# Experts of an attention and mixture kernel in four equal steps, both products in three fp32r parts

## The chip, the cores and the metric

One core of a Trainium2 chip runs the kernel. The metric is device microseconds from launch to end, the median of several executions. TensorE is written PE, VectorE DVE, ScalarE ACT, GpSimd POOL, and SyncE SP in the profile.

## The reference

```python
x = x + cross_attention(layernorm(x), ctx)       # 16 batches, 128 tokens of 512, 2048 context rows
x = x + delta_rule_attention(layernorm(x))       # 4 heads of 128
xr = layernorm(x).reshape(2048, 512)             # mixture of experts
gate = softmax(xr @ Wg); idx = argmax(gate)      # one expert of 16 for each token
dispatched[idx, loc] = xr                        # 128 places for each expert, the rest dropped
h = relu(einsum('ecm,emf->ecf', dispatched, w1)) # 128x512 by 512x2048, for each expert
expert_out = einsum('ecf,efm->ecm', h, w2)       # 128x2048 by 2048x512
x = x + expert_out[idx, loc] * gate[idx]
```

Everything is fp32. The change concerns the two products of the experts. Their weights are 4 MB each for each expert, 128 MB in all.

## The kernel before

The program has two parts. `attention` takes the 16 batches through the two attentions and the routing; it writes each token's normed row, its row of x, its gate and its number to the place of its expert in `dispatched`, in device memory. `experts` then takes the 16 experts one after the other. Each engine runs its own instruction list in program order, written out by hand; they meet at semaphores (`Count.at` gives semaphore and value).

The expert part works in groups g = 0 to 3 of 512 of the 2048 hidden columns. For expert x:

- **SyncE** loads the 128 rows (`dis`, line 1208), w1 in two halves of 2 MB (`load_w1`, line 123) and w2 in two halves (line 1217). Two experts' weights are held, so a load waits for the product of two experts earlier. w1 of expert 0 is loaded inside `attention` already (line 396), into the memory that held context; w2 of expert 0 is not.
- **TensorE** turns the rows (`turn_rows`, line 1232, four fp32 transposes). `up` (line 1243) makes a group of the first product as 16 fp32 matmuls with w1 as the stationary side and the turned rows, 128 columns, as the moving side; each stands as two records in the trace. Its result lies turned already. `down` (lines 1257 to 1259) makes a group of the second product as 12 fp32r matmuls of 512 columns: high part by high part, high by low and low by high, added up in one bank.
- **ScalarE** makes w2h, the high part of a group of w2 (line 1283, 128x2048), and hh, the relu and high part of the first product (line 1289).
- **VectorE** copies the turned rows (line 1304), makes hl, the low part of h (line 1315), half of w2l, the low part of w2 (line 1310, 128x1024), and adds the result to the rows (line 1333).
- **GpSimd** makes the other half of w2l (line 1346, 128x1024) and, at an expert's end, scatters the rows to the output with an indirect DMA (line 1353), behind a one-element operation (line 1352) that carries its waits.

TensorE's order is written out:

```python
up(x, 0)
for g in (1, 2):
    up(x, g)
    down(x, g - 1)
if x + 1 < E:
    turn_rows(x + 1)
up(x, 3)
down(x, 2)
down(x, 3)
```

The transfers of both parts and their order stand in SyncE's lists; `attention`'s SyncE walks over i (batch) and t (128 ticks of a batch).

## Time and profile before

| | us |
|---|---|
| median of three runs | 2172.67 (2171.48 to 2175.91) |
| the profiled execution's own time | 2173.11 |
| its span, first to last instruction | 2171.3 |
| attention part, until the expert part's first instruction | 1746.0 |
| TensorE busy | 2095.7 (97%) |
| GpSimd busy | 1635.7 (75%) |
| VectorE busy | 1272.3 (59%) |
| ScalarE busy | 1220.7 (56%) |
| moved by DMA | 262.31 MB, mean 121 GB/s |

Busy shares are means over two parts that differ much, so the expert part has to be read by itself, in windows. An instruction's time in the trace includes what it waits for inside its engine, for instance for its turn at a memory port. The chain of waits follows the last instruction back to what released it.

### The profile page before, as it was taken

How to read it: one execution, taken by the hardware profiler on the slowest of the kernel's cores; microseconds unless marked ns; L12 is line 12 of the kernel's file. 1: busy time of each engine (PE TensorE's matmuls, PEld its weight loads, DVE VectorE, ACT ScalarE, POOL GpSimd, SP SyncE). 2: the span in 40 equal slices, each digit the busy share in tenths (PEclk: the TensorE clock that was granted, in tenths of full speed). 3: DMA queues.
4: the chain of work that ended last, by engine and by line, in shares of the span. 5: the costliest groups of instructions: out<-in, count | busy, mean ns of one | idle time of the engine just before them, and what ended most of it. 6: DMA issues, size and time to landing. Idle time of an engine off the chain costs nothing. (4 is left out here: it accounts for less than half of the span.)

```text
span 2171.3 us, 35745 instructions
## 1 busy us (share of the span) xinstructions
PE 2095.7 (97%) x12908; PEld 1421.6 (65%) x12908; DVE 1272.3 (59%) x2226; ACT 1220.7 (56%) x2277; POOL 1635.7 (75%) x1387
## 2 busy tenths in 40 slices
PE   7879999999999999999999999999989999999999
PEld 5436565656565656666565656565645789999998
DVE  5656767676666666676767676766664433333332
ACT  3756575666666566666665666666655233433333
POOL 0778888888888888888888888889798145555555
PEclk8989999999999999999999999999999999999999
DMA  4752121212212121212131212112200089999994
GB/s 159 242 113 90 48 74 45 73 52 66 75 48 74 45 73 53 74 44 82 39 97 43 74 43 74 59 57 71 79 15 11 12 313 357 363 352 359 360 348 177
DMA packets 107055, 262.31 MB, mean 121 GB/s; under 512 B 8960, under 2 KB 34304, under 8 KB 98688
## 3 DMA queue, kind: packets, MB, share of 16 engines
q1 hardware_dynamic: 96912, 234.92, 31.6%
q10 hardware_dynamic: 6384, 14.62, 2.3%
q0 software_dynamic: 3584, 10.49, 1.2%
q8 instruction: 103, 1.69, 0.3%
q14 instruction: 72, 0.59, 0.1%
HBM read 223.67 MB, written 25.72 MB: 115 GB/s over the span
## 5 line engine op out<-in xcount | busy, mean ns | idle before, releaser
L1094 POOL TENSOR_TENSOR psum<-psum,weights 128x512 f32<-128x512 f32 x896 | 1152.6, 1286 | 163.4 <-ACT weights L702 60.5
L880 DVE TENSOR_REDUCE mpart<-bank 128x1 f32<-128x512 f32 x1024 | 680.4, 684 | 308.9 <-PE bank L447 300.0
L702 ACT ACTIVATE weights<-bank 128x512 f32<-128x512 f32 x1024 | 597.0, 599 | 324.1 <-PE bank L460 313.3
L460 PE MATMUL bank<-qT,kT 97*128 97x512 f32 x1024 | 482.8, 477 | 10.0 <-DMA qT<-mrow 6.5
L447 PE MATMUL bank<-kT,qT 96*128 96x512 f32 x1024 | 450.0, 451 | 9.6 <-DVE mpart L880 6.8
L447 PEld LDWEIGHTS bank<-kT,qT 96*128 96x128 f32 x1024 | 196.9, 192 | 141.2 <-issue 87.4
L1346 POOL TENSOR_TENSOR w2l<-w,w2h 128x1024 fp32r<-128x1024 f32 x64 | 202.9, 3171 | 75.8 <-PE ebank L1259 54.5
L460 PEld LDWEIGHTS bank<-qT,kT 97*128 97x128 f32 x1024 | 195.7, 193 | 89.4 <-issue 49.2
L472 PE MATMUL bank<-weights,v 128*32 128x512 f32 x2048 | 251.3, 609 | 0.0
L737 ACT COPY w_first<-bank 128x512 f32<-128x512 f32 x248 | 144.7, 584 | 67.6 <-PE bank L412 64.6
L1289 ACT ACTIVATE hh<-ebank 128x512 fp32r<-128x512 f32 x64 | 38.2, 597 | 224.6 <-PE ebank L1243 224.6
L412 PE MATMUL bank<-cst,w_first 128*128 128x128 f32 x992 | 151.5, 276 | 8.3 <-ACT w_first L737 4.7
L412 PEld LDWEIGHTS bank<-cst,w_first 128*128 128x128 f32 x992 | 119.9, 141 | 51.8 <-issue 22.2
L1283 ACT CAST w2h<-w 128x2048 fp32r<-128x2048 f32 x64 | 121.5, 1898 | 43.8 <-DMA w<-in_w 43.8
L472 PEld LDWEIGHTS bank<-weights,v 128*32 128x32 f32 x2048 | 53.7, 110 | 120.2 <-issue 93.8
L538 PE MATMUL bank<-w_first,wkv 128*64 128x512 f32 x512 | 124.0, 605 | 0.0
L1315 DVE SCALAR_TENSOR_TENSOR hl<-ebank,hh 128x512 fp32r<-128x512 f32 x64 | 44.2, 691 | 133.6 <-ACT hh L1289 133.6
L1243 PE MATMUL ebank<-dT,w_first 128*128 128x128 f32 x1024 | 120.2, 278 | 0.9 <-DVE dT L1304 0.9
L1243 PEld LDWEIGHTS ebank<-dT,w_first 128*128 128x128 f32 x1024 | 119.3, 195 | 2.4 <-issue 1.2
L1310 DVE TENSOR_TENSOR w2l<-w,w2h 128x1024 fp32r<-128x1024 f32 x64 | 79.1, 1235 | 71.1 <-PE ebank L1259 48.0
L1243 PEld LDWEIGHTS ebank<-dT,w 128*128 128x128 f32 x1024 | 117.5, 192 | 1.4
L1243 PE MATMUL ebank<-dT,w 128*128 128x128 f32 x1024 | 118.2, 275 | 0.0
(174 smaller groups left out, 3019.3 us busy)
## 6 DMA issues: line engine op xcount, KB each, us to landing
w<-in_w SPq DMA_DIRECT2D x48, 2048.0 KB, 19.9
w_first<-in_ctx SPq DMA_DIRECT2D x62, 1024.0 KB, 5.2
w_first<-in_w SPq DMA_DIRECT2D x16, 2048.0 KB, 12.2
dispatched<-route ACTq DMA_DIRECT2D x17, 513.0 KB, 8.5
dis<-dispatched SPq DMA_DIRECT2D x16, 513.0 KB, 3.5
qT<-qh SPq DMA_DIRECT2D x128, 64.0 KB, 3.4
qT<-qs SPq DMA_DIRECT2D x64, 64.0 KB, 2.1
xr<-in_x SPq DMA_DIRECT2D x16, 256.0 KB, 2.7
```

The source lines that it names most:

```text
L412: ins = e.transpose(out[0:m, j * P:(j + 1) * P], src(j), ident)
L447: e.matmul(a[:], qT[b % 2][0:3 * HD, (4 * g + h) * P:(4 * g + h + 1) * P], kT[b % 2][0:3 * HD, c * 512:(c + 1) * 512], start=True, stop=Tr ...
L460: e.matmul(B_BANK[u % 2][:], kT[b % 2][0:3 * HD + 1, k * P:(k + 1) * P], qT[b % 2][0:3 * HD + 1, g * 512:(g + 1) * 512], start=True, stop= ...
L472: ins = e.matmul(PV_BANK[HD * j:HD * (j + 1), :], v1[b % 2][:, k + j, :], p[(UNITS * b + u + j) % NP], start=k == 0, stop=k == KB - 4)
L538: ins = e.matmul(KV_BANK[rows, :], wkv[:, j, :], cxT[c % 2][:, j, :], start=j < 2, stop=j >= 2)
L702: e.activation(p[n % NP], B_BANK[u % 2][:], ACT.Exp).then_inc(p_act.sem, 1)
L737: e.copy(cxT[c % 2][:, :, kk * P:(kk + 1) * P], turn_bank(b, ("t", k))[:].rearrange("p (c t) -> p c t", c=DC)).then_inc(cxT_act.sem, 1)
L880: e.tensor_reduce(mpart[g % 2][:, 4 * (n % 4) + n // 4:4 * (n % 4) + n // 4 + 1], max_bank(b, g, n)[:], AX.X, ALU.max).then_inc(max_dve.se ...
L1094: e.tensor_tensor(acc[:], first, p[(UNITS * b + u) % NP], ALU.add).then_inc(psum_pool.sem, 1)
L1243: ins = e.matmul(H_BANK[g][:, f * P:(f + 1) * P], w1[q][:, c, (4 * g + f) * P:(4 * g + f + 1) * P], dT[q][:, c, :], start=c == 0, stop=c = ...
L1283: e.copy(w2h[g][:], w2[q][:, 4 * g:4 * g + 4, :]).then_inc(w2h_act.sem, 1)
L1346: e.tensor_tensor(w2l[g % 2][:, 2:4, :], w2[q][:, 4 * g + 2:4 * g + 4, :], w2h[g][:, 2:4, :].bitcast(F32), ALU.subtract).then_inc(w2l_pool ...
```

## The change

The experts run in 64 equal steps s = 4x + g. Both products are made of three fp32r parts now. The first one is the other way round: the turned rows, split in dTh (ScalarE) and dTl (VectorE), are the stationary side and 512 columns of w1 the moving side. So its result has to be turned, by four fp32 transposes for each step (`turn`). For that w1 is split as well, in w1h (ScalarE) and w1l (VectorE, one instruction of 128x2048). h passes through three stages: relu into SBUF (ScalarE), transposes, then hh (ScalarE) and hl (VectorE). Of w2l VectorE makes a quarter (128x512) and GpSimd three quarters, in three instructions.

TensorE does in each step the first product of s, the transposes of s - 1 and the second product of s - 2. Weights are held once, in four parts each, and a part is loaded again when it has been split (line 1230 for w1, 1234 for w2). w1 and w2 are laid out on the host so that each part is 128 rows of 8 KB. w2 of expert 0 is loaded within the last batch's chain into `weights`, the memory of the attention weights, which the expert part keeps as its w2. The rows of an expert come in two loads now, `dis` (what is multiplied) and `rest`; the result is added in `rest`, two steps after the expert's last product.

```diff
+                    if (i, t) == (B, 3):
+                        e.wait_ge(*pv_pe.at(LAST, UNITS // 4 - 1))
+                        e.wait_ge(*psum_pool.at(LAST, 15 * HG - 1))
+                        for g in range(4):
+                            e.dma_start(weights[:, 2048 * g:2048 * (g + 1)], T["w2"][0][g]).then_inc(w2_in[g].sem, 16)
                     if t == LOAD_AT[3] and i == LAST - 1:
                         e.wait_ge(*kv_pe.at(LAST, 3))
-                        for j in (0, 1):
-                            load_w1(e, T, w1_first, 0, j).then_inc(w1_in[j].sem, 16)
+                        for g in range(4):
+                            e.dma_start(w1_first[:, g, :], T["w1"][0][g]).then_inc(w1_in[g].sem, 16)
...
-        T_BANK, H_BANK, Y_BANK = bank[0], bank[1:5], bank[5:7]
-        w1 = [w1_first, sb("w11", [P, DC, F])]
-        w2 = [sb(f"w2{i}", [P, FT, D]) for i in range(2)]
-        dis = [sb(f"dis{i}", [P, ROUTE]) for i in range(2)]
+        T_BANK, U_BANK, HT_BANK, Y_BANK = bank[0], bank[1:3], bank[3:5], bank[5:7]
+        w2 = weights[:, 0:4 * 4 * D].rearrange("p (g n) -> p g n", g=4)
+        w1h, w2h = ([sb(f"{n}{i}", [P, 4, 512], F32R) for i in range(3)] for n in ("w1h", "w2h"))
+        w1l, w2l = ([sb(f"{n}{i}", [P, 4, 512], F32R) for i in range(2)] for n in ("w1l", "w2l"))
...
+        dTh, dTl = ([sb(f"{n}{i}", [P, DC * P], F32R) for i in range(2)] for n in ("dTh", "dTl"))
+        h = [sb(f"h{i}", [P, 512]) for i in range(2)]
+        hh, hl = ([sb(f"{n}{i}", [P, 512], F32R) for i in range(2)] for n in ("hh", "hl"))
...
+            load_rows(0)
+            for s in range(STEPS):
+                x, g = divmod(s, 4)
+                if 4 <= s < STEPS:
+                    e.wait_ge(*w1h_act.at(s - 4))
+                    e.wait_ge(*w1l_dve.at(s - 4))
+                    e.dma_start(w1[:, g, :], T["w1"][x][g]).then_inc(w1_in[g].sem, 16)
+                    e.wait_ge(*w2h_act.at(s - 4))
+                    e.wait_ge(*w2l_dve.at(s - 4))
+                    e.wait_ge(*w2l_pool.at(s - 4, 2))
+                    e.dma_start(w2[:, g, :], T["w2"][x][g]).then_inc(w2_in[g].sem, 16)
+                if g == 2 and x + 1 < E:
+                    load_rows(x + 1)
+                if g == 3:
+                    load_rest(x)
...
+            def up(s):
+                x, g = divmod(s, 4)
+                high, low, out = dTh[x % 2], dTl[x % 2], U_BANK[s % 2]
+                if g == 0:
+                    e.wait_ge(*dT_dve.at(x))
+                if s >= 2:
+                    e.wait_ge(*relu_act.at(s - 2))
+                e.wait_ge(*w1h_act.at(s))
+                e.wait_ge(*w1l_dve.at(s))
+                for c in range(DC):
+                    rows = slice(c * P, (c + 1) * P)
+                    e.matmul(out[:], high[:, rows], w1h[s % 3][:, c, :], start=c == 0, stop=False)
+                    e.matmul(out[:], high[:, rows], w1l[s % 2][:, c, :], start=False, stop=False)
+                    ins = e.matmul(out[:], low[:, rows], w1h[s % 3][:, c, :], start=False, stop=c == DC - 1)
+                ins.then_inc(u_pe.sem, 1)
+            def turn(s):
+                e.wait_ge(*relu_act.at(s))
+                if s >= 2:
+                    e.wait_ge(*hl_dve.at(s - 2))
                 for f in range(4):
+                    ins = e.transpose(HT_BANK[s % 2][:, f * P:(f + 1) * P], h[s % 2][:, f * P:(f + 1) * P], ident[:])
+                ins.then_inc(ht_pe.sem, 1)
+            def down(s):
+                e.wait_ge(*hl_dve.at(s))
+                e.wait_ge(*w2l_dve.at(s))
+                e.wait_ge(*w2l_pool.at(s, 2))
...
-            for x in range(E):
-                up(x, 0)
-                for g in (1, 2):
-                    up(x, g)
-                    down(x, g - 1)
-                if x + 1 < E:
-                    turn_rows(x + 1)
-                up(x, 3)
-                down(x, 2)
-                down(x, 3)
+            for s in range(STEPS + 2):
+                if s % 4 == 2 and s // 4 + 1 < E:
+                    turn_rows(s // 4 + 1)
+                if s < STEPS:
+                    up(s)
+                if 1 <= s <= STEPS:
+                    turn(s - 1)
+                if s >= 2:
+                    down(s - 2)
...
+            def split_w1(s):
+                e.wait_ge(*w1_in[s % 4].at(s // 4))
+                if s >= 3:
+                    e.wait_ge(*u_pe.at(s - 3))
+                e.copy(w1h[s % 3][:], w1_part(s)).then_inc(w1h_act.sem, 1)
+            def split_w2(s):
+                e.wait_ge(*w2_in[s % 4].at(s // 4))
+                if s >= 3:
+                    e.wait_ge(*y_pe.at(s - 3))
+                e.copy(w2h[s % 3][:], w2_part(s)).then_inc(w2h_act.sem, 1)
+            def relu(s):
+                e.wait_ge(*u_pe.at(s))
+                if s >= 2:
+                    e.wait_ge(*ht_pe.at(s - 2))
+                e.activation(h[s % 2][:], U_BANK[s % 2][:], ACT.Relu).then_inc(relu_act.sem, 1)
+            def high(s):
+                e.wait_ge(*ht_pe.at(s))
+                if s >= 2:
+                    e.wait_ge(*y_pe.at(s - 2))
+                e.copy(hh[s % 2][:], HT_BANK[s % 2][:]).then_inc(hh_act.sem, 1)
+            def turned(x):
+                e.wait_ge(*dT_pe.at(x))
+                if x >= 2:
+                    e.wait_ge(*u_pe.at(4 * (x - 2) + 3))
+                e.copy(dTh[x % 2][:], T_BANK[:]).then_inc(dT_act.sem, 1)
+            split_w1(0)
+            split_w1(1)
+            turned(0)
+            for s in range(STEPS + 1):
+                if 0 < s < STEPS - 1:
+                    split_w1(s + 1)
+                if s % 4 == 2 and s // 4 + 1 < E:
+                    turned(s // 4 + 1)
+                if s < STEPS:
+                    relu(s)
+                if s >= 1:
+                    high(s - 1)
+                if s < STEPS:
+                    split_w2(s)
...
+                e.tensor_tensor(dTl[x % 2][:], T_BANK[:], dTh[x % 2][:].bitcast(F32), ALU.subtract).then_inc(
+                    dT_dve.sem, 1)
+            def low_w1(s):
+                e.wait_ge(*w1h_act.at(s))
+                if s >= 2:
+                    e.wait_ge(*u_pe.at(s - 2))
+                e.tensor_tensor(w1l[s % 2][:], w1_part(s), w1h[s % 3][:].bitcast(F32), ALU.subtract).then_inc(
+                    w1l_dve.sem, 1)
+            def low_w2(s):
+                e.wait_ge(*w2h_act.at(s))
+                if s >= 2:
+                    e.wait_ge(*y_pe.at(s - 2))
+                e.tensor_tensor(w2l[s % 2][:, 0:1, :], w2_part(s, 0, 1), w2h[s % 3][:, 0:1, :].bitcast(F32),
+                                ALU.subtract).then_inc(w2l_dve.sem, 1)
+            def low(s):
+                e.wait_ge(*hh_act.at(s))
+                if s >= 2:
+                    e.wait_ge(*y_pe.at(s - 2))
+                e.tensor_tensor(hl[s % 2][:], HT_BANK[s % 2][:], hh[s % 2][:].bitcast(F32), ALU.subtract).then_inc(
+                    hl_dve.sem, 1)
+            def add(x):
+                q = x % 2
+                e.wait_ge(*rest_in[q].at(x // 2))
+                e.tensor_copy(index[q][:], rest[q][:, D + 1:D + 2].bitcast(U32)).then_inc(index_dve.sem, 1)
+                e.wait_ge(*y_pe.at(4 * x + 3))
+                e.scalar_tensor_tensor(rest[q][:, 0:D], Y_BANK[q][:], rest[q][:, D:D + 1], rest[q][:, 0:D],
+                                       ALU.mult, ALU.add).then_inc(eo_dve.sem, 1)
+            low_w1(0)
+            low_w1(1)
             turned(0)
-            for x in range(E):
-                q = x % 2
-                split(x, 0)
-                for g in range(3):
-                    low(x, g)
-                    split(x, g + 1)
-                if x + 1 < E:
-                    turned(x + 1)
-                low(x, 3)
-                if x >= 2:
-                    e.wait_ge(*rows_out[q].at(x // 2 - 1))
-                e.wait_ge(*rows_in[q].at(x // 2))
-                e.tensor_copy(index[q][:], dis[q][:, ROUTE - 1:ROUTE].bitcast(U32)).then_inc(index_dve.sem, 1)
-                e.wait_ge(*y_pe.at(x, 3))
-                e.scalar_tensor_tensor(eo[q][:], Y_BANK[q][:], dis[q][:, 2 * D:2 * D + 1], dis[q][:, D:2 * D],
-                                       ALU.mult, ALU.add).then_inc(eo_dve.sem, 1)
+            for s in range(STEPS + 3):
+                if 0 < s < STEPS - 1:
+                    low_w1(s + 1)
+                if 1 <= s <= STEPS:
+                    low(s - 1)
+                if s < STEPS:
+                    low_w2(s)
+                if s % 4 == 2 and s // 4 + 1 < E:
+                    turned(s // 4 + 1)
+                if s % 4 == 2 and s >= 6:
+                    add(s // 4 - 1)
...
+            for s in range(STEPS + 3):
+                if s < STEPS:
+                    e.wait_ge(*w2h_act.at(s))
+                    if s >= 2:
+                        e.wait_ge(*y_pe.at(s - 2))
+                    for c in (1, 2, 3):
+                        e.tensor_tensor(w2l[s % 2][:, c, :], w2_part(s)[:, c, :],
+                                        w2h[s % 3][:, c, :].bitcast(F32), ALU.subtract).then_inc(w2l_pool.sem, 1)
+                if s % 4 == 2 and s >= 6:
+                    x = s // 4 - 1
...
+                    e.tensor_tensor(pad[:, 0:1], pad[:, 1:2], pad[:, 1:2], ALU.mult).then_inc(hold_pool.sem, 1)
+                    e.indirect_dma_start(
+                        out=T["out"].rearrange("b p d -> (b p) d"),
+                        out_offset=bass.IndirectOffsetOnAxis(ap=index[x % 2][:, 0:1], axis=0), in_=rest[x % 2][:, 0:D],
+                        in_offset=None, bounds_check=B * P - 1, oob_is_err=False).then_inc(rows_out[x % 2].sem, 16)
...
+    w1 = np.ascontiguousarray(g["L0_ffn_w1"].reshape(E, DC, P, 4, 512).transpose(0, 3, 2, 1, 4)).reshape(E, 4, P, 2048)
+    w2 = np.ascontiguousarray(g["L0_ffn_w2"].reshape(E, 4, 4, P, D).transpose(0, 1, 3, 2, 4)).reshape(E, 4, P, 2048)
```

On VectorE, from the middle of the expert part, around an expert's end. Before (w2l is the half of 1024, dT the turned rows, eo the result):

```order
L1315 SCALAR_TENSOR_TENSOR hl<-ebank,hh 128x512 [waits hh_act]
L1310 TENSOR_TENSOR w2l<-w,w2h 128x1024 [waits y_pe2,w2h_act]
L1304 COPY dT<-ebank 128x512 [waits h_pe,dT_pe]
L1315 SCALAR_TENSOR_TENSOR hl<-ebank,hh 128x512 [waits hh_act]
L1331 COPY index<-dis 128x1 [waits rows_in0,rows_out0]
L1333 SCALAR_TENSOR_TENSOR eo<-ebank,dis 128x512 [waits y_pe2]
L1310 TENSOR_TENSOR w2l<-w,w2h 128x1024 [waits y_pe2,w2h_act]
```

After, the same place (w2l is the piece of 512, w1l the 2048 of w1):

```order
L1374 TENSOR_TENSOR w2l<-weights,w2h 128x512 [waits y_pe2,w2h_act]
L1367 TENSOR_TENSOR w1l<-w_first,w1h 128x2048 [waits u_pe,w1h_act]
L1381 TENSOR_TENSOR hl<-ebank,hh 128x512 [waits y_pe2,hh_act]
L1374 TENSOR_TENSOR w2l<-weights,w2h 128x512 [waits y_pe2,w2h_act]
L1360 TENSOR_TENSOR dTl<-ebank,dTh 128x512 [waits u_pe,dT_act]
L1387 COPY index<-rest 128x1 [waits rest_in1]
L1389 SCALAR_TENSOR_TENSOR rest<-ebank,rest 128x512 [waits y_pe2]
L1367 TENSOR_TENSOR w1l<-w_first,w1h 128x2048 [waits u_pe,w1h_act]
```

In each step VectorE has one instruction of 2048 and one of 512 with two SBUF operands where it had one of 1024; dTl takes the place of the copy dT, and the addition stands two steps later.

On ScalarE, at the start of the expert part. Before (w2h is the high part of w2, hh that of h):

```order
L1283 CAST w2h<-w 128x2048 [waits w2_in00]
L1289 ACTIVATE hh<-ebank 128x512 [waits h_pe]
L1283 CAST w2h<-w 128x2048 [waits w2_in00]
L1289 ACTIVATE hh<-ebank 128x512 [waits h_pe]
L1283 CAST w2h<-w 128x2048 [waits w2_in01]
```

After (w1h is the high part of w1, dTh that of the turned rows, h the relu):

```order
L1313 CAST w1h<-w_first 128x2048 [waits w1_in0]
L1313 CAST w1h<-w_first 128x2048 [waits w1_in1]
L1337 CAST dTh<-ebank 128x512 [waits dT_pe]
L1325 ACTIVATE h<-ebank 128x512 [waits u_pe]
L1319 CAST w2h<-weights 128x2048 [waits w2_in0]
L1313 CAST w1h<-w_first 128x2048 [waits w1_in2]
L1325 ACTIVATE h<-ebank 128x512 [waits u_pe]
L1331 CAST hh<-ebank 128x512 [waits ht_pe]
L1319 CAST w2h<-weights 128x2048 [waits w2_in1]
```

Two casts of w1 and the rows' high part now stand ahead of the first relu, and a third cast of w1 behind the first cast of w2.

## Rows read from the trace of the kernel before

**Rows 1.** The chain that ended last, by line, of the page.
```profile
PE ebank L1243 11%; PE ebank L1257 3%; PE ebank L1259 3%; PE ebank L1258 3%; PE ebank L1232 0%; PE ebank L1263 0%; DMA eident<-in_consts 0%; POOLq L1166 0%; DVE dT L1304 0%; POOL pad L1352 0%; POOLq L1353 0%
```

**Rows 2.** Windows: busy us (instructions) of PE, PEld, DVE, ACT, POOL; clock, DMA share, GB/s.
```profile
1800.00:1850.00 50.00, 50.00 (x350) 46.00 (x350) 17.33 (x22) 19.34 (x16) 27.95 (x13) 1.00 0.95 353
1850.00:1900.00 50.00, 50.00 (x350) 46.01 (x349) 16.78 (x22) 19.34 (x16) 28.20 (x12) 1.00 0.97 360
```

**Rows 3.** Timeline of PE in experts 0 and 1: start, duration, instructions.
```profile
1771.47 0.60 PE L1232 MATMUL ebank<-eident,dis 128*128 128x128 f32 x4
1771.90 3.74 PE L1243 MATMUL ebank<-dT,w_first 128*128 128x128 f32 x32
...
1788.01 0.47 PE L1257 MATMUL ebank<-w2h,hh 128*128 128x512 f32 x1
1788.32 0.39 PE L1258 MATMUL ebank<-w2l,hh 128*128 128x512 f32 x1
...
1790.84 3.73 PE L1243 MATMUL ebank<-dT,w 128*128 128x128 f32 x32
1794.33 0.47 PE L1257 MATMUL ebank<-w2h,hh 128*128 128x512 f32 x1
```

**Rows 4.** Timeline: first product of experts 0, 1 and 2, first cast of w2.
```profile
1753.00 9.37 PE L1243 MATMUL ebank<-dT,w_first 128*128 128x128 f32 x64 [0.87 <-DVE dT L1304]
1756.77 1.90 ACT L1283 CAST w2h<-w 128x2048 fp32r<-128x2048 f32 x1 [18.78 <-DMA w<-in_w]
...
1780.94 7.30 PE L1243 MATMUL ebank<-dT,w 128*128 128x128 f32 x64
...
1806.64 7.30 PE L1243 MATMUL ebank<-dT,w_first 128*128 128x128 f32 x64
```

**Rows 5.** Groups by line and form from 1750: busy, mean ns, idle before.
```profile
L1346 POOL TENSOR_TENSOR w2l<-w,w2h 128x1024 fp32r<-128x1024 f32 x64 | 202.9, 3171 | 75.8 <-PE ebank L1259 54.5 <-ACT w2h L1283 21.0
L1283 ACT CAST w2h<-w 128x2048 fp32r<-128x2048 f32 x64 | 121.5, 1898 | 43.8 <-DMA w<-in_w 43.8
...
L1289 ACT ACTIVATE hh<-ebank 128x512 fp32r<-128x512 f32 x64 | 38.2, 597 | 224.6 <-PE ebank L1243 224.6
```

**Rows 6.** Timeline of DVE and POOL, experts 0 and 1.
```profile
1758.70 1.23 DVE L1310 TENSOR_TENSOR w2l<-w,w2h 128x1024 fp32r<-128x1024 f32 x1 [5.86 <-ACT w2h L1283]
...
1758.83 10.03 POOL L1346 TENSOR_TENSOR w2l<-w,w2h 128x1024 fp32r<-128x1024 f32 x3 [12.71 <-ACT w2h L1283]
...
1761.24 2.00 DVE L1310 TENSOR_TENSOR w2l<-w,w2h 128x1024 fp32r<-128x1024 f32 x1 [0.71 <-ACT w2h L1283]
...
1765.41 1.23 DVE L1310 TENSOR_TENSOR w2l<-w,w2h 128x1024 fp32r<-128x1024 f32 x1 [1.57 <-PE ebank L1259]
...
1784.32 2.38 POOL L1346 TENSOR_TENSOR w2l<-w,w2h 128x1024 fp32r<-128x1024 f32 x1
...
1785.34 0.69 DVE L1315 SCALAR_TENSOR_TENSOR hl<-ebank,hh 128x512 fp32r<-128x512 f32 x1 [2.26 <-ACT hh L1289]
...
1791.11 1.23 DVE L1310 TENSOR_TENSOR w2l<-w,w2h 128x1024 fp32r<-128x1024 f32 x1 [1.50 <-PE ebank L1259]
1791.15 3.40 POOL L1346 TENSOR_TENSOR w2l<-w,w2h 128x1024 fp32r<-128x1024 f32 x1 [0.52 <-PE ebank L1259]
```

**Rows 7.** Timeline of POOL in the attention part, two operations of 512 back to back.
```profile
899.01 1.28 POOL L1094 TENSOR_TENSOR psum<-psum,weights 128x512 f32<-128x512 f32 x1
900.25 1.27 POOL L1109 TENSOR_TENSOR qs<-qs,qh 128x512 fp32r<-128x512 f32 x1
```

**Rows 8.** Timeline of the last instructions.
```profile
2165.67 0.39 PE L1259 MATMUL ebank<-w2h,hl 128*128 128x512 f32 x1
...
2166.99 0.19 POOL L1352 TENSOR_TENSOR pad<-pad 128x1 f32<-128x1 f32 x1 [6.41 <-issue]
2167.72 0.99 POOL L1353 DMA_INDIRECT out<-eo,index  x1 [0.54 <-issue]
```

**Rows 9.** The window with the lowest rate among those of 10 us.
```profile
1802.00:1812.00 10.00, 10.00 (x71) 9.16 (x70) 3.32 (x5) 3.50 (x3) 4.10 (x3) 1.00 0.81 267
```

151 lines of the change are left out of this document (44 added, 107 removed).

## The prediction

> **What bounds the kernel now.** I read the chain of waits first. Its last 19% of the span are all TensorE work of the expert part [rows 1]: the chain goes through the lines 1243 (first product) and 1257 to 1259 (second product) and through nothing else of weight. The windows say the same: from 1800 to 1900 TensorE is busy 50.00 of 50 us at granted clock 1.00 (the 2.4 GHz level), while ScalarE has 19 us and VectorE 17 us of work, GpSimd 28 us, and the DMA engines stand at 0.95 of their time with 353 to 360 GB/s [rows 2]. So TensorE sets the time; GpSimd and the transfers come next. The attention part is not touched up to the last batch's chain, so the whole change is decided between 1746 us and the end, 425 us.
>
> The timeline gives the unit prices [rows 3]. A group of the first product (16 fp32 matmuls, 32 records) goes from 1790.84 to 1794.33: 3.49 us. A group of the second product (12 fp32r matmuls) goes from 1788.01 to 1790.84: 2.83 us, and from its second matmul on one costs (1790.84 - 1788.32) / 11 = 0.229 us. The four transposes of an expert's rows take 1771.90 - 1771.47 = 0.43 us. Per expert that is 4 x (3.49 + 2.83) + 0.43 = 25.7 us, and the first products of experts 1 and 2 stand 25.70 us apart [rows 4]: TensorE never waits.
>
> **TensorE after the change.** A step has 12 fp32r matmuls for the first product (12 x 0.229 = 2.75), four fp32 transposes of h (0.43) and the second product as before (2.83): 6.01 us. With the rows' transposes and one more change of type (0.08) an expert costs 24.55 us, 1.15 less than now. Sixteen experts: -18.4 us. That is the whole gain on offer.
>
> **The first w2, loaded early.** Today w2 of expert 0 is issued only when the expert part begins, and ScalarE starts on it at 1756.77 [rows 4]. It looks like a stall, but expert 0 took 27.9 us (1753.00 to 1780.94) against 25.7, and 9.37 - 7.30 = 2.07 us of that is the clock: its first 64 records ran partly at the lower level. Left is 0.2 us. The 4 MB move into an idle stretch, and I cost them at that 0.2 us gain. Their new wait in SyncE's queue stands at step 3 after the last batch's start, behind the load of xr and ahead of the last store only, so nobody else waits for it.
>
> **ScalarE.** Per step two casts of 2048 (1.90 each) and two moves of 512 (0.60 each) [rows 5]: 5.0 us, with the rows' high part 5.2. It fits in 6.01, and it is no longer idle much. I cost it at nothing in the steady part, where TensorE covers it; at the start it counts (below).
>
> **VectorE and GpSimd together.** Here the traces speak against the change. A difference on GpSimd of 128x1024 takes 2.38 us alone, even while VectorE makes hl beside it from a PSUM and an SBUF operand (1784.32 and 1785.34). Beside VectorE's own difference of two SBUF operands (1791.11) it takes 3.40 us: 1.02 more. Three in a row with three of VectorE's take 10.03, 0.96 more each, and VectorE's second one, begun inside GpSimd's, took 2.00 instead of 1.23 [rows 6]. So the two engines' SBUF-with-SBUF operations take turns. Of the 64 GpSimd operations the mean is 3171 ns [rows 5]; today that is free, because the sum, 3.2 to 3.4 us a step, lies far under 6.32.
>
> The change puts more on this pair. GpSimd gets three pieces of 512 instead of one of 1024: back to back such operations start 1.24 us apart [rows 7], so 3.72 us. VectorE gets w1l, 2048 elements in one instruction, and a 512 piece of w2l. By 1.02 us for each 1024 elements they hold GpSimd up for 2.04 + 0.51. The sum is 6.27 us a step, over TensorE's 6.01 and ScalarE's 5.0, and it is one chain through GpSimd's queue. Each expert adds the scatter of its rows, 0.19 + 0.99 us and the gaps around them [rows 8], 1.3 us; VectorE may use that time. Bounds for an expert are thus 4 x 6.27 = 25.1 (all beside) and 26.4 (nothing beside). I take 26.2, since VectorE is then mostly at work that needs PSUM only. Either end is near the 25.7 of today and above 24.55: the gain on TensorE can't be cashed in. With w2l and the high parts of w2 double and triple buffered, TensorE soon stands at the second product, waiting for GpSimd's last piece.
>
> The Trainium skill ("SBUF — State Buffer", Who interferes with whom) says more: the port pair is an exclusive lock, held for the whole instruction. By that rule the full durations add up, not 1.02 but 1.23 for each 1024; the rows show the shorter turn, and I go by them, but the rule is a rival below.
>
> **The start.** Work before the first product grows. ScalarE casts two parts of w1 (1746.2 to 1750.0), VectorE makes w1l of both (2.31 each, by 0.69 for 512 and 1.23 for 1024) until 1752.8, then dTl until 1753.5. The first matmul comes at 1753.6 instead of 1753.00. It pays the same 2.07 us for the low clock: up(0) ends at 1758.4, up(1) at 1761.2. Then relu(0), the cast of w2 and the third cast of w1 end at about 1763.1, and VectorE's w1l(2) has to wait for one piece of GpSimd's: it ends at about 1766.5, so TensorE idles 4.5 us. The first second-product group starts at 1769.7; GpSimd is done with step 0 at 1767.6. This pipeline is two steps deep, where the present one is one deep.
>
> **The end.** From 1767.6 GpSimd makes 61 steps of 6.27 (382.5), two without any w1l beside them (2 x 4.23 = 8.5) and 15 scatters at 1.1 (16.5): 2175.1. The last group adds 2.83, and from the last matmul's end to the end of the span it is 2171.3 - 2166.06 = 5.2 us [rows 8]. Span 2183.2; the profiled execution's time lies 1.8 above its span (2173.1 to 2171.3), so **2185 us**, 12 more than the profiled 2173.1 and the median 2172.67. If every scatter lies beside VectorE's work, 16.5 less: 2168.5. If the turns cost 0.2 us more a step, 12 more: 2197.
>
> A measurement of this kernel can tell about 0.2%, 4.3 us, from no change: under 2168.3 is faster, over 2177.0 slower.
>
> **Rivals.**
> - *TensorE still bounds.* If the turns cost less than the rows say (the pieces are shorter and fall between VectorE's work), an expert costs 24.55. From 1769.7: 61 steps of 6.14 (374.5), then 2.83 + 0.43 + 2.83 + 2.83 to 2153.1, plus 5.2 and 1.8: 2160, faster by 0.6%. Against it: 6.27 has to fall by 0.13 and the scatter has to vanish, while all rows of the collision agree within 0.06. It decides from the point at which the pair's sum falls under 6.14. Chance 0.15.
> - *Scatters beside, turns as measured.* 2168 to 2177, no change that can be told. Chance 0.17.
> - *Full durations.* No overlap when the turn passes over: 3 x 1.27 + 2.31 + 0.69 = 6.81 a step, 0.54 more, times 61: 33 more, 2218. Against it the 0.96 and 1.02 of [rows 6]; for it that one 2048-wide instruction and four hand-overs a step are in no row. Chance 0.10. It is what the rule of the Trainium skill quoted above gives.
> - *Transfers late.* SyncE issues w1 of the next step behind w2, whose wait now includes GpSimd's last piece four steps earlier. From there until ScalarE wants that w1 it is at least one down, one up, relu, high and a cast: 2.83 + 2.75 + 0.6 + 0.6 + 1.9 = 8.7 us, for 2.1 MB. At 353 GB/s [rows 2] they need 5.9, at the lowest window's 267 GB/s [rows 9] 7.9. Over 8.7 each 0.5 us costs 30: 2215. An expert moves 9.2 MB, in 26.2 us 350 GB/s, which the rows show as possible. Chance 0.08.
> - *The change doesn't do what it says.* The instruction order shows that it does, on every engine; nothing is left for this.
>
> **How the numbers follow.** The forecast (2177 to 2200, likeliest 2185) has 0.50. Slower: 0.50 + 0.10 + 0.08 = 0.68; same 0.17; faster 0.15. The range takes in the forecast with both bounds and the TensorE case, and leaves out most of the last two: 2158 to 2212.
>
> **What would show it.** In the new profile: GpSimd's 512 pieces at a mean of (3.72 + 2.55) / 3 = 2.1 us instead of 1.27, GpSimd without idle in the expert part, and w1l on VectorE longer than 2.31, as it waits in its turn. Experts 26.2 us apart. TensorE's idle time ahead of the second product, ended by GpSimd's w2l, or ahead of the first, ended by w1l; its busy share in 50 us windows 46 to 48. DMA share under 1. Start of the first product 1753.6, and some 4 us idle after its second group. Wrong would be: GpSimd pieces near 1.3 us with TensorE at 50 of 50 (first rival), idle time ended by a DMA (fourth), or a first group that starts much later than 1754.

## The result and the profile after

| | before | after |
|---|---|---|
| device time, median of four runs, us | 2172.07 (2171.23 to 2175.91) | 2224.38 (2222.56 to 2226.83) |
| ratio, 95% interval | | 1.024 (1.0226 to 1.0254) |
| span of the profiled execution, us | 2171.3 | 2220.8 |

The change makes the kernel 2.4% slower, 52 us. The forecast was slower, but 2185 and at most 2212.

The windows of the new kernel, the same two stretches as in [rows 2] and in the same columns:

```profile
1800.00:1850.00 50.00, 46.45 (x211) 37.29 (x210) 40.26 (x26) 35.14 (x32) 44.23 (x25) 0.97 0.83 318
1850.00:1900.00 50.00, 43.05 (x193) 34.56 (x192) 39.99 (x26) 31.39 (x28) 38.55 (x25) 0.93 0.83 312
```

TensorE had 50.00 of 50 before and has now 46 and 43, and its granted clock was 0.97 and 0.93 over the two windows, where it was 1.00 (the 2.4 GHz level) before: it fell at times to the lower level. That much was forecast in kind (46 to 48). But the pair VectorE and GpSimd, which should have been the bound, is not full either: GpSimd stands at 38.55 of 50. The DMA share fell from 0.97 to 0.83. Nothing is full, so the engines wait for each other. The groups from 1800 to 2150 (busy, mean ns of one, idle before, releaser), which answer to [rows 5]:

```profile
L1418 POOL TENSOR_TENSOR w2l<-weights,w2h 128x512 fp32r<-128x512 f32 x145 | 258.9, 1820 | 60.3 <-PE ebank L1290 59.9
L1367 DVE TENSOR_TENSOR w1l<-w_first,w1h 128x2048 fp32r<-128x2048 f32 x50 | 138.1, 2761 | 13.0 <-ACT w1h L1313 13.0
L1374 DVE TENSOR_TENSOR w2l<-weights,w2h 128x512 fp32r<-128x512 f32 x49 | 97.5, 1990 | 45.2 <-PE ebank L1290 44.8
...
L1265 PE MATMUL ebank<-w1h,dTh 128*128 128x512 f32 x196 | 83.2, 425 | 36.9 <-DVE w1l L1367 36.9
```

Two rows should catch the eye. VectorE's piece of w2l (L1374) has the same size as any of GpSimd's three and takes 0.69 us when nothing is in its way, yet its mean is 1990 ns; its tile's line, with minimum, median and maximum in ns over all 64, shows that a few take 11.2 us. And TensorE's idle time (36.9 us) is ended by w1l, which VectorE makes right behind that piece.

```profile
L1374 DVE TENSOR_TENSOR w2l<-weights,w2h x64: 674/920/11209, 1757.9 to 2205.5; 128x512 fp32r<-128x512 f32 x64
```

The timelines of VectorE and GpSimd (start, duration, what; idle time before it) show one of the places. GpSimd:

```profile
1859.11 2.24 POOL L1426 TENSOR_TENSOR pad<-pad 128x1 f32<-128x1 f32 x1
1861.50 1.00 POOL L1427 DMA_INDIRECT out<-rest,index  x1
1862.52 11.20 POOL L1418 TENSOR_TENSOR w2l<-weights,w2h 128x512 fp32r<-128x512 f32 x9
1884.82 6.38 POOL L1418 TENSOR_TENSOR w2l<-weights,w2h 128x512 fp32r<-128x512 f32 x3 [11.11 <-PE ebank L1290]
```

VectorE, and the first matmul of the group behind it:

```profile
1861.22 0.68 DVE L1381 TENSOR_TENSOR hl<-ebank,hh 128x512 fp32r<-128x512 f32 x1
1863.06 11.21 DVE L1374 TENSOR_TENSOR w2l<-weights,w2h 128x512 fp32r<-128x512 f32 x1 [1.16 <-PE ebank L1290]
1874.19 2.28 DVE L1367 TENSOR_TENSOR w1l<-w_first,w1h 128x2048 fp32r<-128x2048 f32 x1
```
```profile
1876.62 0.77 PE L1265 MATMUL ebank<-w1h,dTh 128*128 128x512 f32 x1 [6.69 <-DVE w1l L1367]
```

VectorE asks for its turn at 1863.06 and, since the difference itself takes 0.69 us, gets it at about 1873.6, after nine pieces of GpSimd, which run at 1.25 us each, undisturbed. No turn is passed: VectorE comes in when GpSimd has nothing left. Behind it w1l is late, TensorE stands idle for 6.69 us, and GpSimd, which ran ahead, then idles for 11.11 us. The clock pays too, as two windows behind the idle spell show (0.62, then 1.00):

```profile
1876.00:1882.00 6.00, 5.38 (x18) 4.33 (x19) 3.87 (x4) 0.52 (x2) 0.00 (x0) 0.62 0.99 410
1882.00:1888.00 6.00, 6.00 (x30) 4.86 (x29) 3.91 (x6) 4.64 (x5) 3.18 (x3) 1.00 0.64 268
```

There are seven such instructions: one that takes 6.5 us at 1808.6, and six that take 11.2 us, at 1863.1, 1921.4, 1979.7, 2037.8, 2095.8 and 2153.9; 0.69 us of each is the work itself, so the waits are 5.8 and 10.5 us. The additions that end the experts (L1389) stand 24.6 us apart without one and 33.4 to 33.8 us with one, so each costs 8.9 us: 6.7 idle and 2.2 by the clock. Together with 5.0 for the first they make 5.0 + 53.5 = 58.5 us, and 2220.8 - 58.5 = 2162.3, 9 us under the span before. **In the account of this trace, all of the loss stands behind these seven waits.** That is not what a kernel without them would take: during a long wait GpSimd makes nine pieces at 1.25 us instead of some 2.1, and has caught up behind it, so that an expert of 24.6 us can follow. *e9_gap* below has no long wait and takes 2193. (That *e4_all_dve*, another sharing of the work, has a span of 2162.3 too is chance.)

Why is only every second expert hit? In the others, VectorE's w1l comes 0.27 to 0.30 us after the DMA has begun and gets in at once, ahead of GpSimd's pieces, and the later requests wait for one piece at most. VectorE, then GpSimd, of such a place:

```profile
1892.24 2.29 DVE L1367 TENSOR_TENSOR w1l<-w_first,w1h 128x2048 fp32r<-128x2048 f32 x1 [0.50 <-ACT w1h L1313]
```
```profile
1891.95 0.99 POOL L1427 DMA_INDIRECT out<-rest,index  x1 [0.15 <-issue]
1892.96 9.05 POOL L1418 TENSOR_TENSOR w2l<-weights,w2h 128x512 fp32r<-128x512 f32 x4
```

In six of the experts that are hit, w1l has ended 0.2 us before the DMA, and VectorE's next request for w2l comes 1.56 to 1.59 us after the DMA's start. In the first one w1l runs into the DMA, which lasts 2.97 us, and the request comes 4.61 us after its start.

### The profile page after: what moved, and what is told of

Same layout as the page of the kernel before. It is cut to its first block and busy times, and to the rows that moved or that the text cites. A ratio compares the mean times of both kernels' runs of the same rounds, so it can differ in the third digit from the quotient of the medians.

```text
span 2220.8 us, 34559 instructions
## 1 busy us (share of the span) xinstructions
PE 2093.7 (94%) x11884; PEld 1369.4 (62%) x11884; DVE 1491.1 (67%) x2290; ACT 1373.6 (62%) x2421; POOL 1790.0 (81%) x1515
## 5 line engine op out<-in xcount | busy, mean ns | idle before, releaser
L1418 POOL TENSOR_TENSOR w2l<-weights,w2h 128x512 fp32r<-128x512 f32 x192 | 342.7, 1820 | 86.7 <-PE ebank L1290 72.1
L1367 DVE TENSOR_TENSOR w1l<-w_first,w1h 128x2048 fp32r<-128x2048 f32 x64 | 176.6, 2761 | 23.2 <-ACT w1h L1313 23.1
L1374 DVE TENSOR_TENSOR w2l<-weights,w2h 128x512 fp32r<-128x512 f32 x64 | 121.7, 1902 | 67.2 <-PE ebank L1290 59.6
L1265 PE MATMUL ebank<-w1h,dTh 128*128 128x512 f32 x256 | 109.8, 429 | 50.4 <-DVE w1l L1367 47.7
L1325 ACT ACTIVATE h<-ebank 128x512 f32<-128x512 f32 x64 | 38.3, 598 | 152.5 <-PE ebank L1267 152.5
L1313 ACT CAST w1h<-w_first 128x2048 fp32r<-128x2048 f32 x64 | 122.6, 1917 | 8.6 <-PEq L122 8.0
L1319 ACT CAST w2h<-weights 128x2048 fp32r<-128x2048 f32 x64 | 123.1, 1923 | 0.0
L1093 POOL TENSOR_TENSOR psum<-weights 128x512 f32<-128x512 f32 x64 | 83.5, 1305 | 39.0 <-ACT weights L701 37.6
L1287 PE MATMUL ebank<-w2h,hh 128*128 128x512 f32 x256 | 107.3, 419 | 3.7 <-POOL w2l L1418 3.7
```

What stands on the lines that cost most here:

```text
L1093: e.tensor_tensor(acc[:], first, p[(UNITS * b + u) % NP], ALU.add).then_inc(psum_pool.sem, 1)
L1319: e.copy(w2h[s % 3][:], w2_part(s)).then_inc(w2h_act.sem, 1)
L1367: e.tensor_tensor(w1l[s % 2][:], w1_part(s), w1h[s % 3][:].bitcast(F32), ALU.subtract).then_inc(w1l_dve.sem, 1)
L1418: e.tensor_tensor(w2l[s % 2][:, c, :], w2_part(s)[:, c, :], w2h[s % 3][:, c, :].bitcast(F32), ALU.subtract).then_inc(w2l_pool.sem, 1)
```

## Experiments

Theory at the start: VectorE's difference, when it meets GpSimd's, is normally let in after one piece, but in some place it is shut out until GpSimd's queue is empty. Rivals: the pair is overloaded as such (a backlog), the transfers, or the pieces that follow each other without a gap. All kernels below are the changed one but for the edit shown. Ratios are to the kernel before on the same chip, with 95% intervals; the differences in us between kernels of different rows are between medians, partly of different chips.

**1. The scatter, left out.** *e1_one_scatter* leaves out the scatter of experts 0 to 14 (their rows do not reach the output) with its waits and product; *e5_wait_only* leaves out the same scatters, but keeps GpSimd's waits and the product. The edit of the second:

```
-                    e.indirect_dma_start(out=..., in_=rest[x % 2][:, 0:D], ...)
+                    if x == E - 1:
+                        e.indirect_dma_start(...)
```

Expected of the first: 

> The scatters of experts 0 to 14 are left out (so their rows of the output keep the value without the experts); only the last one is made. Theory backlog (GpSimd's queue falls behind TensorE's 6.04 us step, mostly by the scatters, and when VectorE asks for its piece of w2l while more than a step of GpSimd's pieces is queued it is not let in until the queue is empty): without scatters GpSimd falls behind by 0.1 us a step only, so at most one or two waits over 5 us are left of the seven, each worth 8.9 us; 2157 to 2170 us. Theory scatter (the indirect DMA itself sets the state in which VectorE is not let in): no such wait, 2157. Theory sum (the prediction: the pair's turns add up to 6.27 us a step): 2170 to 2175, GpSimd without idle time.

Expected of the second: 

> The changed kernel without the indirect DMA for experts 0 to 14: their rows are not scattered, but GpSimd's waits for the add and its one-element product stay where they are. If the DMA itself makes the long waits: none of the seven, and GpSimd bound as in e1_one_scatter, 2168 to 2175 us. If it is the pause and the free start after it, DMA or not: long waits of 6 to 11 us remain and the time stays above 2205 us.

Measured: 2170.38 us, ratio 0.9976 (0.9964 to 0.9988), and 2172.03, ratio 0.9988 (0.9979 to 0.9997). No difference on VectorE takes over 3.5 us in either. The window and GpSimd's group of *e5_wait_only*:

```profile
1850.00:1900.00 50.00, 49.19 (x231) 39.43 (x230) 43.99 (x30) 38.01 (x34) 50.00 (x26) 1.00 0.93 356
```
```profile
L1417 POOL TENSOR_TENSOR w2l<-weights,w2h 128x512 fp32r<-128x512 f32 x168 | 345.5, 2095 | 0.0
```

This is the pair as it was forecast: GpSimd without idle time, its pieces at a mean of 2.095 us (forecast 2.1), 12 x 2.095 = 25.1 us an expert. The time and GpSimd's full window are those of the sum theory, the missing long waits those of the scatter theory, whose 2157 us did not come. The backlog is there and harmless. It is the DMA that makes the long waits, not the pause before it. With the fifteen DMAs of 1.0 us, the kernel takes 52 us more.

**2. How the work is shared.** VectorE takes two, three or four of the four pieces of w2l in one instruction, GpSimd the rest.

```
-                e.tensor_tensor(w2l[s % 2][:, 0:1, :], w2_part(s, 0, 1), w2h[s % 3][:, 0:1, :].bitcast(F32),
+                e.tensor_tensor(w2l[s % 2][:, 0:2, :], w2_part(s, 0, 2), w2h[s % 3][:, 0:2, :].bitcast(F32),
...
-                    for c in (1, 2, 3):
+                    for c in (2, 3):
```

Two (*e2_half*): 

> VectorE makes two of the four pieces of w2l in one instruction of 1024, GpSimd two of 512, all scatters stay. The turns add up to 2 x 1.24 + 2.04 + 1.02 = 5.54 us a step, under TensorE's 6.04. Theory backlog: GpSimd has 0.5 us a step to spare and catches up after each scatter, no wait over 5 us, TensorE busy without gaps, about 2157 us. Theory scatter: long waits of VectorE's w2l stay behind the scatters, over 2190. Theory sum: 2157 as well.

Three (*e3x_dve3*): 

> VectorE makes three of the four w2l pieces in one 128x1536 instruction and GpSimd one. GpSimd has then never more than one or two pieces behind a scatter, since its queue runs dry each step: a request that meets the DMA waits for two pieces at most, 2.6 us, where e2_half showed 3.1 and the changed kernel 11.2. VectorE has 2.28 + 1.75 + 0.69 = 4.7 us a step plus hand-overs. Shut-out theory: under 3 us each, covered by the two steps of slack, so TensorE bound like e4_all_dve, 2164 to 2170 us. If two pieces more or less make no difference to the waits, 2179 as e2_half.

Four (*e4_all_dve*): 

> VectorE makes all of w2l in one instruction of 2048, GpSimd only scatters. VectorE's own sum is 2 x 2.31 + 0.69 + 0.37 = 5.7 us a step, under 6.04. All theories: no turn to wait for, TensorE bounds, the idle 4 us behind the second step at the start get shorter; 2152 to 2158 us. If it is over 2165, VectorE's own chain bounds.

| VectorE's pieces | time, us | ratio | longest wait |
|---|---|---|---|
| 1 (the change) | 2224.38 | 1.024 (1.0226 to 1.0254) | 10.5 |
| 2 | 2179.17 | 1.0016 (1.0007 to 1.0025) | 3.1, twelve times |
| 3 | 2162.75 | 0.9946 (0.9931 to 0.9961) | 1.1 |
| 4 | 2165.13 | 0.9955 (0.9940 to 0.9970) | none |

The 2179.17 of *e2_half* fits neither of its forecasts (2157, or over 2190): the long waits are there, but short. Less stands in GpSimd's queue; the request comes 0.32 us into the DMA and again passes behind everything that GpSimd has, here two pieces. VectorE and GpSimd:

```profile
1856.58 4.32 DVE L1374 TENSOR_TENSOR w2l<-weights,w2h 128x1024 fp32r<-128x1024 f32 x1
```
```profile
1856.26 1.00 POOL L1427 DMA_INDIRECT out<-rest,index  x1
1857.28 2.53 POOL L1418 TENSOR_TENSOR w2l<-weights,w2h 128x512 fp32r<-128x512 f32 x2
```

With three or four pieces on VectorE there is no such wait, and both are some 0.5% faster than the kernel before. So the fp32r form is worth having; it is the sharing of w2l that spoils it. With four, both differences run undisturbed (mean 2284 and 2291 ns), VectorE has 43.5 of 50 us. Its 2165.13 us missed the forecast of 2152 to 2158: 3.4 us of TensorE's idle time at the start stayed, and its experts stand 24.86 us apart where those of *e3x_dve3* stand 24.59. Why is not shown; VectorE is not full.

*e3x_dve3* does not only have a shorter wait than forecast, it has none, and that is an exception to what follows. Its request for w2l comes 0.55 us into the DMA, with one piece of GpSimd's behind, and gets in at once (1.76 us, undisturbed), fourteen times here and fourteen in *e11_dve3_start*. VectorE, then GpSimd, whose piece waits instead:

```profile
1855.51 1.76 DVE L1374 TENSOR_TENSOR w2l<-weights,w2h 128x1536 fp32r<-128x1536 f32 x1 [0.15 <-PE ebank L1290]
```
```profile
1854.96 0.99 POOL L1427 DMA_INDIRECT out<-rest,index  x1 [0.15 <-issue]
1855.97 2.45 POOL L1418 TENSOR_TENSOR w2l<-weights,w2h 128x512 fp32r<-128x512 f32 x1
```

GpSimd's piece waits for the same matmul (L1290) as VectorE's, 0.4 us into the DMA; in the changed kernel and in *e2_half* it was released before the DMA began. Whether that makes the difference, no run tests.

**3. A gap behind every piece.** *e3_gaps* puts a one-element memset on GpSimd behind each of its pieces, to break up the run.

```
                         e.tensor_tensor(w2l[s % 2][:, c, :], ...).then_inc(w2l_pool.sem, 1)
+                        e.memset(gap[:, 3 * s + c - 1:3 * s + c], 0.0)
```

> A one-element memset stands behind each of GpSimd's pieces (192 more instructions on the busier engine, 0.1 us each), nothing else changes. If VectorE is shut out because GpSimd's pieces follow each other without a gap (each begins before the one ahead has ended), the memset, which reads no SBUF, opens the turn: no wait of VectorE's w2l over 2 us, and the kernel gets faster though GpSimd has more to do; 2170 to 2185, now by the sum of 6.27 + 0.3 a step. If the backlog decides without regard to gaps, the waits of 10.5 us stay or come more often: 2225 to 2235.

Measured: 2234.03 us, ratio 1.0266 (1.025 to 1.0281), with seven differences of 11.6 us, as before. A memset between the pieces is no opening. GpSimd starts the memset before the piece ahead has ended and the next piece before the memset has (0.05 us after its start), so the edit made no gap: an instruction that does not read SBUF is still work in the queue.

**4. The wait by itself.** Two kernels without any of the computation repeat one encounter many times. GpSimd runs six 128x512 differences back to back; VectorE asks for one at a moment that a copy on ScalarE sets.

```
for i, (k, w) in enumerate(TRIALS):          # GpSimd
    e.wait_ge(*start.at(i))
    if "p" in k or "d" in k:  e.tensor_tensor(pad[:, 0:1], pad[:, 1:2], pad[:, 1:2], ALU.mult)
    if "d" in k:              e.indirect_dma_start(out=..., in_=zero[:], ...)
    for c in range(6):        e.tensor_tensor(outp[:, c, :], src[:, c % 4, :], high[:, c % 4, :]..., ALU.subtract)
```

> This kernel leaves the whole computation out and only measures one thing: 36 trials, one after the other. In each GpSimd makes six 128x512 differences of two SBUF operands back to back (1.25 us apart, as in the changed kernel), and VectorE asks for one such difference at a set moment, released by a copy on ScalarE whose width is swept from 0.2 to 1.9 us. Kinds: nothing ahead of the pieces; the one-element product ahead; the product and an indirect DMA of 128 rows ahead; the same with a hl-like operation of VectorE (PSUM and SBUF operands) before its request. Theory 'fresh after the scatter': VectorE's 0.69 us piece waits for one piece at most (under 1.3 us) in the first two kinds, and for all that GpSimd has queued (up to 6 pieces, 7.5 us) where the indirect DMA is ahead and the request falls into the DMA or the first piece after it. Rival 'any free run of GpSimd': VectorE is shut out for all the remaining pieces whenever GpSimd took the port without waiting, in the first kinds too, up to 7 us. Rival 'something else in the expert part' (semaphores, the other engines, DMA traffic): no wait over 1.3 us in any trial.

> The computation is left out here too: 27 trials like those of m1_offsets, but VectorE first makes a 128x2048 difference (w1l's form, 2.28 us), which GpSimd's first operation runs into and waits for, then a hl-like one, then asks for its 128x512 piece between 2.3 and 4.2 us after the start. Kinds: six pieces alone; the one-element product and six pieces; product, indirect DMA and six pieces, which is the order seen before each long wait of the changed kernel. Theory 'fresh after the scatter': waits of one piece at most in the first two kinds, since GpSimd had to wait itself and hands over after it; in the third, requests in the DMA or the first piece behind it wait until GpSimd's queue is empty, 4 to 7 us. Rival 'any free run': long waits in all three kinds when the request falls into the second piece or later, since that piece was taken without waiting. Rival 'something else': no wait over 1.3 us.

Two trials of *m1_offsets* side by side, the request 0.25 us and 0.51 us into the DMA (VectorE's operation is L239, ScalarE's L175):

```profile
198.01 0.99 POOL L203 DMA_INDIRECT out<-zero,index  x1 [0.53 <-POOL pad L198]
198.26 0.69 DVE L239 TENSOR_TENSOR part<-src,high 128x512 fp32r<-128x512 f32 x1 [1.06 <-ACT slow L175]
199.03 7.35 POOL L209 TENSOR_TENSOR outp<-src,high 128x512 fp32r<-128x512 f32 x6
...
217.03 0.99 POOL L203 DMA_INDIRECT out<-zero,index  x1 [0.53 <-POOL pad L198]
217.54 8.40 DVE L239 TENSOR_TENSOR part<-src,high 128x512 fp32r<-128x512 f32 x1 [1.32 <-ACT slow L175]
218.04 7.35 POOL L209 TENSOR_TENSOR outp<-src,high 128x512 fp32r<-128x512 f32 x6
```

217.54 + 8.40 = 225.94 is 0.55 us after the end of the last piece at 225.39: all six passed. And a trial without the DMA, where the turn is passed after one piece:

```profile
106.92 7.81 POOL L209 TENSOR_TENSOR outp<-src,high 128x512 fp32r<-128x512 f32 x6
107.22 1.51 DVE L239 TENSOR_TENSOR part<-src,high 128x512 fp32r<-128x512 f32 x1 [0.52 <-ACT slow L175]
```

Over both kernels, 29 trials without a DMA gave waits of at most 1.10 us (two of them asked before GpSimd had begun). Of 34 with one, the 16 whose request came at 0.31 us into it or earlier waited 0.06 us at most; the 18 at 0.38 us or later, up to the first piece, waited 7.0 to 7.8 us. A collision of GpSimd with a wide operation of VectorE ahead of the DMA, or a hl-like operation beside it, changes nothing. Both rivals fall: a free run of GpSimd alone shuts nobody out, and the effect needs none of the rest of the kernel.

**5. What ends it.** *m3_release* adds later requests, a semaphore wait on GpSimd between the DMA and the pieces, and a memset there.

> The computation is left out; 24 trials as in m1_offsets, six 128x512 pieces on GpSimd behind an indirect DMA, to find what ends the shut-out that the two kernels before showed (requests later than 0.38 us into the DMA waited 7 to 7.9 us, until all six pieces were done). Kinds: requests up to 3.3 us after the start, in the second and third piece behind the DMA; GpSimd waiting on a semaphore between the DMA and the pieces, with a gap from none to about 0.9 us; a 128x1024 memset on GpSimd in that place; and late requests without any DMA. Theory 'GpSimd keeps the port from the DMA on until it stands idle': late requests with no gap wait for all that is left of the six pieces; with a gap, however short, they wait for one piece at most (1.3 us); the memset, being work of GpSimd, does not help. Rival 'the DMA only shields the first pieces': late requests get in after one piece, with or without a gap. Rival 'it lasts until the rows have landed': the gap changes nothing, and the wait ends at a fixed time after the DMA.

Two trials. In the first the semaphore is there before the DMA ends, in the second a little after (GpSimd's pieces are L223, VectorE's L253):

```profile
67.94 0.99 POOL L209 DMA_INDIRECT out<-zero,index  x1 [0.53 <-issue]
...
68.95 7.36 POOL L223 TENSOR_TENSOR outp<-src,high 128x512 fp32r<-128x512 f32 x6
69.65 7.21 DVE L253 TENSOR_TENSOR part<-src,high 128x512 fp32r<-128x512 f32 x1 [2.52 <-ACT slow L181]
...
77.79 0.99 POOL L209 DMA_INDIRECT out<-zero,index  x1 [0.53 <-issue]
...
78.83 7.81 POOL L223 TENSOR_TENSOR outp<-src,high 128x512 fp32r<-128x512 f32 x6
79.20 1.44 DVE L253 TENSOR_TENSOR part<-src,high 128x512 fp32r<-128x512 f32 x1 [2.22 <-ACT slow L181]
```

From 68.93 to 68.95 there are 0.02 us, as in the trials without a semaphore, and VectorE waits 6.5 us; from 78.78 to 78.83 there are 0.05 us and it waits 0.76. All twelve trials with a gap, 0.05 us or longer, waited 0.76 us at most; the five with requests in the pieces and no such gap waited until the sixth piece was done, also where the request came in the second piece. Of the four trials with the memset behind the DMA, two requests later than its start waited 7.6 and 7.2 us, so it does not help; one at 0.34 us into the DMA got in at once, as the early ones did above; one at 0.04 us into the memset got in at once too, and that one stays unexplained.

**6. Back in the kernel.** *e7_wait_w2l* was to keep GpSimd behind VectorE's w2l of the next step; *e9_gap* puts a certain gap behind each scatter, a memset and a wait for it; *e10_half_gap* does so in *e2_half*.

```
 e7:                 e.indirect_dma_start(...).then_inc(rows_out[x % 2].sem, 16)
+                    if s + 1 < STEPS:
+                        e.wait_ge(*w2l_dve.at(s + 1))
 e9, e10:            e.indirect_dma_start(...).then_inc(rows_out[x % 2].sem, 16)
+                    e.memset(gap[:, x:x + 1], 0.0).then_inc(gap_pool.sem, 1)
+                    e.wait_ge(*gap_pool.at(x))
```

> The changed kernel with one wait more: after each scatter GpSimd waits for VectorE's w2l of the next step before its own three pieces, so that VectorE's request never meets a busy GpSimd there. If the shut-out after the DMA is the whole loss, the seven waits of 6 to 11 us are gone and GpSimd's sum sets the time: per expert 24.55 us of turns as in e5_wait_only plus the DMA 1.0 and about 1.2 us of waiting, against 24.6 to 25.9 us, so 2168 to 2190 us. If the long waits have another cause, they stay and the time is over 2215.

> The changed kernel with a one-element memset on GpSimd behind each scatter and a wait of GpSimd for that memset, so that its queue surely stands still for some hundredths of a microsecond. If the port is held from the DMA until such a gap, and that is the whole miss: all of the long waits go (no VectorE difference over 3.5 us), GpSimd is busy without idle, and the time is that of e5_wait_only (2172) plus up to 16 x 1.25 us for the DMA and the gap: 2172 to 2192, with the prediction's 2185 inside. If the gap must be longer than this, the waits stay and the time is 2220 or more.

> The same gap in e2_half, which had twelve waits of 3.1 us beyond a turn. If the gap frees the port: those waits are gone, and TensorE, which had 48.4 of 50 us there, gets back up to 1.6 us in 50: 2179 less 8 to 12, so 2165 to 2172. If not, 2179 again.

*e7_wait_w2l* changed nothing, 2226.66 us, ratio 1.0234 (1.0219 to 1.0249). The timeline of VectorE says why:

```profile
1860.84 0.94 DVE L1374 TENSOR_TENSOR w2l<-weights,w2h 128x512 fp32r<-128x512 f32 x1 [0.18 <-PE ebank L1290]
...
1866.88 11.17 DVE L1374 TENSOR_TENSOR w2l<-weights,w2h 128x512 fp32r<-128x512 f32 x1 [1.20 <-PE ebank L1290]
```

GpSimd is so far behind that the piece it was told to wait for is the one of 1860.84, done before the scatter at 1865.29; the one shut out belongs to the step after. The wait was already satisfied behind the first fourteen scatters and made no gap there. So this run does not test the remedy it was meant to be; it only shows that a satisfied wait does nothing. It has one thing more: at 1954.26 a w1l that came 0.304 us into the DMA was shut out too (6.69 us instead of 2.29), while those at 0.298 us and earlier, here and in the changed kernel, got in.

*e9_gap* makes a gap of 0.09 us for certain. GpSimd, and the window of both stretches together, of this kernel:

```profile
1861.07 0.99 POOL L1428 DMA_INDIRECT out<-rest,index  x1 [0.15 <-issue]
1862.06 0.12 POOL L1432 MEMSET gap<- 128x1 f32 x1
1862.27 10.11 POOL L1419 TENSOR_TENSOR w2l<-weights,w2h 128x512 fp32r<-128x512 f32 x5
```
```profile
1800.00:2150.00 350.00, 331.75 (x1525) 267.63 (x1524) 258.35 (x198) 254.06 (x224) 340.69 (x197) 0.98 0.90 342
```

The time falls from 2224 to 2193.10 us, 1 us above the 2172 to 2192 expected, ratio 1.0087 (1.0073 to 1.0101), no wait of VectorE is over 1.15 us, and GpSimd is busy for 340.69 of 350 us. So the gap takes back 31 of the 52 us, and the kernel stays 18 us over the kernel before. In *e10_half_gap* the twelve waits are gone and the time falls from 2179 to 2167.64, ratio 0.9965 (0.9952 to 0.9978). One memset and one wait more per expert make both kernels faster. In *e10_half_gap* the requests come 0.31 to 0.32 us into the DMA as in *e2_half*, where twelve of fourteen were shut out; here all fourteen got in at once.

**7. The start, and the early load of w2.** *e8_start* is *e4_all_dve* with the third cast of w1 and the first of w2 ahead of the first relu on ScalarE, *e11_dve3_start* the same on *e3x_dve3*. *e6_late_w2* and *e12_dve3_start_late* undo the early load of w2 on *e4_all_dve* and on *e11_dve3_start*.

```
 e8, e11:    turned(0)
+            split_w1(2)
+            split_w2(0)
 e6, e12:    load_rows(0)
+            for g in range(4):
+                e.dma_start(w2[:, g, :], T["w2"][0][g]).then_inc(w2_in[g].sem, 16)
```

> e4_all_dve with another order on ScalarE at the start: the third cast of w1 and the first cast of w2 come ahead of the first relu, where ScalarE stands idle for some 5 us. If TensorE's 3.4 us of idle time after its second group comes from ScalarE's order there, they go: 3 to 4 us less than e4_all_dve (2165.1), 2161 to 2162 us. If the low clock of the first groups or the transfer of w1 sets that moment, no change.

> e3x_dve3 (VectorE three pieces of w2l, GpSimd one) with the start of e8_start. Steady part at TensorE's pace in both; the start gained 4.2 us on e4_all_dve. Sum of both: 2158 to 2161. If GpSimd's one piece keeps w1l(2) or w2l(0) waiting at the start, half of that gain goes: 2161 to 2163.

> Undoes one part on top of e4_all_dve, which has no long waits: w2 of expert 0 is loaded when the expert part begins, in four parts after the first rows, instead of during the last batch's chain. The prediction put that part at 0.2 us. Here the first cast of w2 stands behind relu(0), about 11 us after the expert part begins, and the first part of w2 (1 MB) lands some 4 to 6 us after its issue: 0 to 2 us longer than e4_all_dve (2165.1). If instead the loads of w2 and of w1 of expert 1 run into each other, w1 comes late and it costs 5 us or more.

> e11_dve3_start with w2 of expert 0 loaded when the expert part begins. With the first cast of w2 now ahead of the first relu, ScalarE waits for that transfer (1 MB lands some 4 to 6 us after its issue, behind the first rows), which is about when the third cast of w1 ends: 0 to 3 us slower than e11_dve3_start. If the load is worth nothing even here, the same time within 0.2%.

*e8_start*: 2160.96 us, ratio 0.9938 (0.9925 to 0.9951), 4.2 us less than *e4_all_dve* (another chip; the intervals of the ratios just overlap). The 3.42 us in which TensorE waited for w1l(2) became 0.7. *e11_dve3_start*: **2157.58 us, ratio 0.9919 (0.9906 to 0.9933), the fastest of all.** Its window:

```profile
1800.00:2150.00 350.00, 350.00 (x1650) 284.32 (x1649) 320.24 (x212) 268.07 (x238) 200.23 (x87) 1.00 0.91 350
```

TensorE is busy throughout, and its experts stand 24.59 us apart. The late load costs 1.1 us on *e4_all_dve* (2166.26, ratio 0.9961, 0.9948 to 0.9975) and 1.8 us on *e11_dve3_start* (2159.42, ratio 0.9931, 0.9916 to 0.9947). The intervals overlap, so all that can be said is that the early load is worth little, some 1 to 2 us by the medians, and perhaps nothing.

## Why the prediction was right and wrong

The direction was right and the size was not: 2224 against 2185, outside the range by 12 us. The direction is not luck: *e9_gap*, which has none of the long waits, is slower than the kernel before too, by 18 us. By its steps:

**TensorE's new work: right.** 6.01 us a step and 24.55 an expert were forecast; undisturbed experts take 24.6 here, and 24.59 in *e11_dve3_start*. Per expert 25.69 - 24.59 = 1.10 us are gained, 17.6 in sixteen, against 18.4 forecast. That kernel is 17.7 us under the kernel before (2175.25, same chip) with its better start; *e3x_dve3*, which lacks that start, is 11.8 us under it (2174.53).

**The early load of w2 at 0.2 us: not refuted**, 1.1 and 1.8 us by medians whose intervals overlap. **ScalarE at nothing: right** in the steady part: with VectorE's waits out of the way (*e11_dve3_start*) TensorE has no idle time that a cast ends. **The start: right.** Up to 4.5 us idle ahead of the third group were forecast, 4.13 are there, behind w1l. The first product began at 1750.80 in this execution and at 1752.9 to 1756.3 in eight others; 1753.6 was forecast.

**The sum of the turns: right as a mean.** 1.02 us for each 1024 elements of VectorE's gave 6.27 us a step and pieces of 2.1 us; *e5_wait_only* shows 2.095 and experts 25.22 us apart, against 25.1 forecast without scatters. The rival of full durations, 6.81 a step, would have made them 27.2. Where turns are passed, the measurement decides for the shorter price. That rival was the prediction's estimate by the rule of the Trainium skill ("SBUF — State Buffer", Who interferes with whom) that the pair of ports is an exclusive lock for the whole instruction.

**The step that failed** is the one on the scatter: "Each expert adds the scatter of its rows, 0.19 + 0.99 us and the gaps around them [rows 8], 1.3 us; VectorE may use that time." It priced the DMA as a piece of GpSimd's time and took for granted that the pair alternates one instruction at a time behind it as everywhere else. In its place the runs show that, where GpSimd has pieces ready behind the DMA, a request of VectorE's which comes more than about 0.3 us into the DMA, or in the pieces behind it, is not served until GpSimd's queue stands still, here up to nine pieces and 10.5 us later. This part of the miss is 2224 - 2193 = 31 of the 39 us. The kernel before has the same DMA once per expert and never met this: its longest VectorE difference there is 2.0 us [rows 6]. GpSimd has one piece a step there and 27.95 of 50 us of work [rows 2], so no long run stands behind the DMA, and VectorE's next request comes 3.84 to 3.90 us after the DMA's start, when the one piece behind it is done. So these traces could not show the wait. In the changed kernel GpSimd needs 24.55 us for its twelve pieces between two long waits, as much as TensorE's whole expert, and the scatter comes on top, so its queue falls behind VectorE's requests until one of them lands behind a scatter; the long wait then empties the queue. The alternation follows from where the requests fall, as shown above; that the backlog sets those moments is my reading, and no run tests it.

**What the sum lacked besides.** With the gap in place the kernel takes 2193, 8 us over the 2185 and inside the range. An expert takes 26.8 us on average (321.3 for twelve, from 1824.7 to 2146.0) against 26.2. In its sum one term was mis-sized: the scatter's one-element product (pad) at 0.19 us. That is the time of the last one [rows 8], which has nothing beside it. The line of all sixteen in the kernel before, minimum, median and maximum in ns, already says 1.05 us:

```profile
L1352 POOL TENSOR_TENSOR pad<-pad x16: 193/1049/1091, 1782.0 to 2167.0; 128x1 f32<-128x1 f32 x16
```

In *e9_gap* it takes 0.65 and 2.24 us by turns, as it waits for VectorE's w2l or w1l. From its start to the first piece it is 2.00 and 3.59 us, 2.8 on average, of which 0.2 is the added gap, where 1.3 were forecast. In return the pieces take less than the 25.1. TensorE's idle spells of some 3 us, ended by GpSimd's w2l, are followed by the lower clock, which the sum had only at the start (window 1841 to 1847, behind one that ends at 1841.51):

```profile
1841.00:1847.00 6.00, 5.49 (x14) 4.25 (x15) 0.00 (x0) 1.80 (x1) 4.07 (x4) 0.50 0.72 264
```

In the changed kernel the clock adds 2.2 us to each 6.7 us idle. No run separates these terms in the last 8 us.

**The rivals.** TensorE bound at 2160 is near what three or four pieces on VectorE give (2158 to 2165), but not this sharing. Late transfers did not come: ScalarE waited for a DMA for 0.2 us from 1800 to 2150. The rival that came true, an engine shut out over many instructions, was not on the list. Two of the signs that the prediction asked for were missing and told of it at once: GpSimd had idle time, and its pieces were at 1.82 us instead of 2.1. None of the signs that it listed as wrong came.

## What to carry to other kernels

Where VectorE and GpSimd both make differences of two SBUF operands, price not only the sum but the longest run in GpSimd's queue behind an indirect DMA. Keep that queue short behind it, or give it a certain gap (a small operation and a wait for it: 31 us here, 12 us in *e2_half*). Price the small operation that carries the waits too, with the median of its line and not with the last one. A wait that is already satisfied is no gap, and neither is a memset alone. A group whose mean (1990 ns) lies far over its undisturbed duration (690 ns) and over its median (920) is the sign of such rare, long waits; look at its longest one before adding up means.

## What the runs showed of the hardware

- Behind an indirect DMA on GpSimd, a VectorE difference of two SBUF operands waited for all that GpSimd had queued: 7.0 to 7.8 us behind six pieces, 3.1 behind two, up to 10.5 in the kernel. The border lies about 0.3 us into the DMA: in the small kernels requests up to 0.31 us got in at once and those from 0.38 us on did not; in *e2_half* twelve at 0.32 us were shut out and two at 0.31 us were not; in *e7_wait_w2l* one at 0.304 us was shut out. Without a DMA no wait was over 1.10 us in 29 trials.
- There are exceptions. With a memset next in GpSimd's queue, requests at 0.34 us (*m3_release*) and at 0.31 to 0.32 us (*e10_half_gap*) got in, and one at 0.04 us into the memset; with a single piece that was released only 0.4 us into the DMA, requests at 0.55 us got in (*e3x_dve3*, *e11_dve3_start*). What holds the port, and what decides these cases, is not shown; the runs only show when it opens. Only indirect DMAs were tried.
- The other way round, an indirect DMA waits for VectorE's difference. It takes 0.99 us alone and took 2.97 us in the changed kernel at 1803.97, where w1l had begun 0.2 us before it; both there and in three trials of *m1_offsets* (1.13, 1.28 and 1.41 us) it ended 0.87 to 0.88 us after VectorE's operation.
- The Trainium skill ("SBUF — State Buffer", Who interferes with whom) says that the pair of ports is held for a whole instruction and that whoever issues first goes first. The trials without a DMA agree (one piece at most). Those with one do not: VectorE issued ahead of five or six of the pieces and went last.
- An operation of VectorE that reads PSUM and SBUF (hl) took 0.68 to 0.69 us each time beside GpSimd's DMA and pieces, in the kernel (64 times) and in *m2_collide* (27 times).
- After an idle spell of 6.69 us TensorE's granted clock was 0.62 over the next 6 us, and 1.00 after that: 2.2 us lost each time. In *e9_gap* it was 0.50, the lower level (1.2 GHz), in the window around the end of a spell of 3.18 us.
